# The net's weights are scanned in 88 pieces inside the attention units, from the inputs, and copied one matrix per chunk

## The chip, the cores and the metric

The kernel runs on one core of a Trainium2 chip. The metric is the time of the whole program in device microseconds; lower is better. The kernel uses four compute engines (PE for matmuls, DVE for vector work, ACT for activations, POOL for small vector work) and SP, which issues most DMAs in program order.

## What is computed

One transformer layer on x of 4096 x 256 in float32, 16 heads of 16 columns:

```python
q, k, v = x @ Wq.T + bq, x @ Wk.T + bk, x @ Wv.T + bv     # 16 heads of 16
q, k = rope(q), rope(k)
x = layernorm(x + softmax(q @ k.T / sqrt(256)) @ v @ Wo.T)
h = silu((x @ w1.T) * s1) * ((x @ w2.T) * s2)              # 256 -> 1024
h = gelu((h @ h1.T) * hs1)                                 # 1024 -> 1024
h = gelu((h @ h2.T) * hs2)                                 # 1024 -> 1024
x = layernorm(x + (h @ w3.T) * s3)                         # 1024 -> 256
```

The weights w1, w2, h1, h2 and w3 hold small whole numbers. The net has a fast form for weights whose low 12 bits are all zero and another for weights of any kind; the kernel looks at all the weights to choose.

## The kernel before

It has three blocks: `project`, `attend` and `feed_forward`. `attend` is the one that changes. It works in 32 units, u = c * NG + g: 8 chunks c of 512 queries times 4 groups g of 4 heads. One unit has 32 steps kt of 128 keys each.

PE does in a step, in this order (`unit`, L550): a pair of score matmuls (L572), two groups of "wide" matmuls (L507), another pair of score matmuls, and the sums over values of the step before (L532). The wide groups are not of the same unit: they compute scores of a later unit, from which DVE takes the maxima (L646), 64 groups (n = 0 to 63) a unit, two a step. `groups_beside` (L539) puts them LEAD = 6 steps ahead: beside step kt of unit u stand groups 2(kt + 6) and 2(kt + 6) + 1 of unit u + 1, and from kt = 26 on those of unit u + 2. A wide group n uses PSUM buffer n % 2 and waits (L504) until DVE has reduced group n - 2. Ahead of unit 0 PE computes all 64 groups of unit 0 and the first 12 of unit 1 with nothing beside them (L580 to L585).

After 64 groups DVE takes the top of each row (L655). PE turns it (L515), ACT negates it into `shift` (L617), POOL splits it (L474 to L485) and SP writes it as extra rows of `q_sb` (`place_shift`, L406), so that the score matmul subtracts the maximum. ACT takes exponentials of the scores (L624) and after the fourth of a unit copies the sums of the unit before to `mixed` (`take_sums`, L603).

Beside the attention the weights are looked through. SP first copies the five matrices to one DRAM buffer `w_dram` (L431, L432) and waits for all (L433). For each unit it loads a 32nd of it, 128 x 704 words, into `w_words` (`load_words`, L435), and DVE ORs the low bits into `bits` behind the unit's top reduction (`scan`, L662). At the end `bits` is reduced to `low_bits` (L680). `feed_forward` loads the weights from `w_dram` (L823).

SP's order in `attend` is: loads of q and of the last keys; two loads that fill the ones rows of `k_all` (L430, 384 KB each, 3 partitions each); the copies; `load_words(0)`, `place_shift(0)`; and then for each unit u:

```python
load_words(u + 1)       # waits for scan(u)
place_shift(u + 1)      # waits for POOL, near the end of unit u
finish(u)               # waits for ACT's take_sums(u), early in unit u + 1
load_q(c + 1, g)        # six DMAs; not in the last chunk
```

Of the kernel before, what the change touches and what calls it, by code (L numbers as in the profile page):

```python
# [19 lines left out]
I32 = mybir.dt.int32  # L20
ALU = mybir.AluOpType
# [3 lines left out]
P = 128  # L25
# [4 lines left out]
NCH = S // CH  # L30
# [7 lines left out]
LOW_BITS = 0xFFF  # L38


W_SHAPES = {"w1T": (D, HID), "w2T": (D, HID), "h1T": (HID, HID), "h2T": (HID, HID), "w3T": (HID, D)}
W_AT, W_TOTAL = {}, 0
for _name, (_rows, _cols) in W_SHAPES.items():
    W_AT[_name] = (W_TOTAL, _rows, _cols)
    W_TOTAL += _rows * _cols
INV_SCALE = 1.0 / float(D) ** 0.5


# [11 lines left out]
def place_k(sp, k_parts, k_all, c, ft, done):  # L60
    cols = bass.ds(c * CH, CH)
    pairs = slice(ft * PAIRS // FT, (ft + 1) * PAIRS // FT)
    for e in range(PAIR):
        for r, part in enumerate(K_PART):
            src = k_parts[part].rearrange("(j e d) s -> e d j s", e=PAIR, d=HD)[e]
            at = e * HALF + r * HD
            sp.dma_start(k_all[at:at + HD, pairs, cols].bitcast(F32), src[:, pairs, cols]).then_inc(done, 16)


def place_q(sp, q_parts, q_sb, c, g, done):  # L70
    for e in range(PAIR):
        for r, part in enumerate(Q_PART):
            src = q_parts[part].rearrange("(j e d) s -> e d j s", e=PAIR, d=HD)[e]
            at = e * HALF + r * HD
            sp.dma_start(q_sb[at:at + HD].bitcast(F32), src[:, g * GP:(g + 1) * GP, bass.ds(c * CH, CH)]).then_inc(done, 16)
# [251 lines left out]
def attend(nc, io, q_parts, k_parts, heads_dram, w_dram, low_bits, v_all, k_all):  # L327
# [6 lines left out]
    with ExitStack() as ctx:  # L334
        def sb(name, shape, dt=F32):
            return ctx.enter_context(nc.sbuf_tensor(name, shape, dt))

        def psum(name, shape):
            return ctx.enter_context(nc.psum_tensor(name, shape, F32))

        def sem(name):
            return ctx.enter_context(nc.semaphore(name))
# [6 lines left out]
        UNITS = NCH * NG  # L349
# [12 lines left out]
        shift_rest = sb("shift_rest", [QT, P])  # L362
        shift_parts = sb("shift_parts", [QT, 3, P], BF16)
        shift_rows = sb("shift_rows", [QT, 3, P], F32R)
        SCAN = W_TOTAL // P // UNITS
        w_words = sb("w_words", [P, SCAN], I32)
        bits = sb("bits", [P, SCAN], I32)
        scores = [psum(f"scores{b}", [P, CH]) for b in range(BANKS)]
        wide = [psum(f"wide{b}", [P, 2, CH]) for b in range(2)]
        sums = psum("sums", [P, CH])  # L370
# [9 lines left out]
        first_turn = sem("first_turn")  # L380
# [4 lines left out]
        exps_done = sem("exps_done")  # L385
        probs_free = sem("probs_free")
        w_copied = sem("w_copied")
        words_in = sem("words_in")
        scanned = sem("scanned")
        sums_free = sem("sums_free")  # L390
        mixed_free = [sem(f"mixed_free{p}") for p in range(2)]

        GROUPS = MAXG // KT

        def slot(n, turn=True):

            return n + 1 if turn and n >= TURN_AT else n
# [3 lines left out]
        @block.sync  # L401
        def _(sp):
            def load_q(c, g):
                place_q(sp, q_parts, q_sb[g], c, g, q_in[g])

            def place_shift(u, g):  # L406

                sp.wait_ge(part_step, (u + 2) * ROUNDS)
                for e in range(PAIR):
                    for a in range(3):  # L410
                        at = e * HALF + SHIFT_ROW + a
                        row = q_sb[g][at:at + 1].rearrange("o j (t s) -> o (j t) s", t=TT)
                        sp.dma_start(row.bitcast(F32), shift_rows[e * GP * TT:(e + 1) * GP * TT, a].bitcast(F32)).then_inc(shift_in, 16)

            def finish(c, g):

                sp.wait_ge(sums_free, c * NG + g + 2)
                sp.dma_start(heads_dram[bass.ds(c, 1), :, g].rearrange("c p s -> (c p) s"), mixed[g % 2][:])\
                    .then_inc(mixed_free[g % 2], 16)

            load_q(0, 0)
            place_k(sp, k_parts, k_all, NCH - 1, FT - 1, k_in)
            for g in range(1, NG):
                load_q(0, g)
            sp.wait_ge(ones_set, 1)
            for e in range(PAIR):
                at = e * HALF + SHIFT_ROW
                rows = k_all[at:at + 3].rearrange("a j (c s) -> a (j c) s", s=CH)
                src = mixed[0][0:3].unsqueeze(1).to_broadcast([3, PAIRS * NCH, CH])
                sp.dma_start(rows.bitcast(F32), src).then_inc(k_ones, 16)  # L430
            for name, (at, rows, cols) in W_AT.items():  # L431
                sp.dma_start(w_dram[at:at + rows * cols].rearrange("(r c) -> r c", c=cols), io[name]).then_inc(w_copied, 16)  # L432
            sp.wait_ge(w_copied, 16 * len(W_AT))  # L433

            def load_words(u):  # L435

                sp.wait_ge(scanned, u + 1)
                words = w_dram.bitcast(I32).rearrange("(u p n) -> u p n", u=UNITS, p=P)[bass.ds(u, 1)]
                sp.dma_start(w_words[:], words.rearrange("u p n -> (u p) n")).then_inc(words_in, 16)

            load_words(0)
            place_shift(0, 0)
            with sp.Fori(0, NCH - 1) as c:
                for g in range(NG):
                    load_words(c * NG + g + 1)
                    place_shift(c * NG + g + 1, (g + 1) % NG)
                    finish(c, g)
                    load_q(c + 1, g)
            for g in range(NG):
                if g < NG - 1:  # L450
                    load_words((NCH - 1) * NG + g + 1)
                    place_shift((NCH - 1) * NG + g + 1, g + 1)
                finish(NCH - 1, g)
            for p in range(2):
                sp.wait_ge(mixed_free[p], 16 + 16 * UNITS // 2)

        @block.gpsimd
        def _(pool):
# [37 lines left out]
        def _(pe):  # L496
# [42 lines left out]
            def groups_beside(c, g, kt, left):  # L539
# [7 lines left out]
                kt = (kt + LEAD) % KT  # L547
                return [(c, g, n) for n in range(kt * GROUPS, (kt + 1) * GROUPS)]

# [30 lines left out]
            for n in range(MAXG):  # L580
                max_group(0, 0, n)
            for n in range(LEAD * GROUPS):
                max_group(0, 1, n)
# [13 lines left out]
        def _(act):  # L597
# [12 lines left out]
            def unit(c, g, first=False, last=False):  # L610
                u = c * NG + g
                for n in range(TILES):
# [7 lines left out]
                    if n % HG == 0:  # L620

                        act.wait_ge(probs_free, u * KT + n // HG + 1)
                    act.wait_ge(scored, u * SLOTS + s + 1)
                    act.activation(probs[n % RING][:], scores[s % BANKS][:], ACT.Exp, scale=INV_SCALE)\  # L624
                        .then_inc(exps_done, 1)
# [11 lines left out]

        @block.vector
        def _(dve):
            def maxima(u):  # L640

                if not (isinstance(u, int) and u == 0):
                    dve.wait_ge(top_ready, u)
                for n in range(MAXG):
                    dve.wait_ge(wide_ready, u * MAXG + n + 1)
                    dve.reduce_max(group_max[:, n], wide[n % 2][:], AX_X).then_inc(wide_free, 1)  # L646
                dve.wait_ge(wide_free, (u + 1) * MAXG + 2)

                if isinstance(u, int):
                    if u == 1:  # L650
                        dve.wait_ge(first_turn, 1)
                else:
                    dve.wait_ge(scored, (u - 2) * SLOTS + TURN_AT + 1)
                by_head = group_max[:].rearrange("q (r b) e -> q e r b", b=NCH)
                dve.reduce_max(top[:].rearrange("q (e r) -> q e r", e=PAIR), by_head, AX_X).then_inc(top_ready, 1)  # L655

            for p in range(2):
                dve.sem_inc(mixed_free[p], 16)
            dve.sem_inc(wide_free, 2)
            dve.sem_inc(shift_in, 96)  # L660

            def scan(u):  # L662

                dve.wait_ge(words_in, u * 16 + 16)
                dve.wait_ge(scanned, u + 1)
                dve.scalar_tensor_tensor(out=bits[:], in0=w_words[:], scalar=LOW_BITS, in1=bits[:],
                                         op0=ALU.bitwise_and, op1=ALU.bitwise_or).then_inc(scanned, 1)

            dve.memset(bits[:], 0).then_inc(scanned, 1)
            maxima(0)  # L670

            dve.memset(sums[:], 0.0).then_inc(sums_free, 1)
            scan(0)
            maxima(1)
            scan(1)
            with dve.Fori(2, UNITS) as u:
                maxima(u)
                scan(u)
            dve.wait_ge(scanned, UNITS + 1)
            dve.reduce_max(low_bits[:], bits[:], AX_X).then_inc(scanned, 1)  # L680
            dve.wait_ge(scanned, UNITS + 2)


def feed_forward(nc, io, heads_dram, shares_dram, w_dram, low_bits, out):
# [562 lines left out]
```

## Time and profile before

| | us |
|---|---|
| median of 3 runs (3811.04 to 3815.56) | 3811.35 |
| the profiled execution | 3821.48 |
| its span, first to last instruction | 3819.9 |
| PE busy | 3526.6 (92%) |
| DVE busy | 2932.8 (77%) |
| ACT busy | 2462.1 (64%) |
| POOL busy | 196.4 (5%) |
| mean granted clock of PE | 0.948 |

In a row of the page or of a list of groups, "L646 DVE TENSOR_REDUCE group_max<-wide" is a line of the kernel, the engine, the operation, and what it writes and reads; then come the shapes, the count, the busy time, the mean of one in ns, and the idle time of the engine just before it with what ended it. A timeline is a list of instructions in order of time, several of a kind merged into one row. PEld is PE's weight load, SPq and POOLq are the queues' own issuing of DMAs. A granted clock of 1.00 is 2.4 GHz, 0.50 is 1.2 GHz.

### The profile page before, as it was taken

Reading aid. Unit: us, or ns where it says so; the run is one execution under the profiler, and the core shown is the slowest. Engines: PE = TensorE matmul, PEld = TensorE weight load, DVE = VectorE, ACT = ScalarE, POOL = GpSimd, SP = SyncE. Lnnn points to the kernel's source line nnn. Section 1 sums busy time; section 2 is a strip of 40 time slices with the busy share of each in tenths; the row PEclk is TensorE's granted clock in tenths of the full one; section 3 lists DMA queues with packets and bytes.
Section 4 is the critical chain, followed back from the end, with each engine's and each line's share of the span. In section 5 each row is a group of like instructions: output and inputs, shape, how many; then the busy total and the mean of one; then the engine's idle time right before and its main releaser. Section 6 shows DMA issues by size and latency. Waiting matters only on the chain. (4 is left out here: it accounts for less than half of the span.)

```text
span 3819.9 us, 63480 instructions
## 1 busy us (share of the span) xinstructions
PE 3526.6 (92%) x20130; PEld 1516.0 (40%) x20130; DVE 2932.8 (77%) x3148; ACT 2462.1 (64%) x4472; POOL 196.4 (5%) x352
## 2 busy tenths in 40 slices
PE   8569999999999999999999999999998869999999
PEld 3223333333333333332333333333332158888887
DVE  6698999899899989998998999899983035555554
ACT  2118888788888878888887888788886512222222
POOL 3200000000000000000000000000000011111100
PEclk9759999999999999999999999999997589999999
DMA  8940000000000000000000000000000051111100
GB/s 208 212 137 12 12 12 12 13 12 12 23 12 12 12 13 12 12 12 17 18 12 13 12 12 12 12 12 23 8 8 4 3 182 35 34 34 44 40 17 12
DMA packets 64516, 125.61 MB, mean 33 GB/s; under 512 B 12551, under 2 KB 24904, under 8 KB 63032
## 3 DMA queue, kind: packets, MB, share of 16 engines
q1 hardware_dynamic: 59528, 114.02, 10.6%
q0 software_dynamic: 4704, 7.81, 0.7%
q8 instruction: 177, 2.90, 0.3%
q14 instruction: 107, 0.88, 0.1%
HBM read 90.59 MB, written 41.16 MB: 34 GB/s over the span
## 5 line engine op out<-in xcount | busy, mean ns | idle before, releaser
L646 DVE TENSOR_REDUCE group_max<-wide 128x2 f32<-128x1024 f32 x2048 | 2406.0, 1219 | 277.9 <-PE wide L507 277.6
L624 ACT ACTIVATE probs<-scores 128x512 f32<-128x512 f32 x4096 | 2223.3, 595 | 524.6 <-PE scores L572 431.5
L572 PE MATMUL scores<-q_sb,k_all 51*128 51x512 f32 x4096 | 1053.5, 511 | 148.6 <-ACT probs L624 62.7
L532 PE MATMUL sums<-probs,v_all 128*17 128x512 f32 x8192 | 1117.7, 619 | 0.0
L572 PEld LDWEIGHTS scores<-q_sb,k_all 51*128 51x128 f32 x4096 | 391.7, 188 | 1384.3 <-ACT probs L624 1355.7
L507 PE MATMUL wide<-k_all,q_sb 48*128 48x512 f32 x4096 | 807.3, 459 | 76.3 <-DVE group_max L646 50.2
L507 PEld LDWEIGHTS wide<-k_all,q_sb 48*128 48x128 f32 x4096 | 397.9, 191 | 394.8 <-DVE group_max L646 363.8
L1029 ACT ACTIVATE whole_hid<-acc,scale 128x512 f32<-128x512 f32 x128 | 84.6, 688 | 346.8 <-PE acc L910 346.7
L910 PE MATMUL acc<-hid_b,h2T 128*128 128x512 f32 x1024 | 241.6, 397 | 0.0
L910 PE MATMUL acc<-hid_a,h1T 128*128 128x512 f32 x1024 | 240.2, 395 | 0.0
L532 PEld LDWEIGHTS sums<-probs,v_all 128*17 128x17 f32 x8192 | 137.4, 96 | 258.2 <-ACT probs L624 150.7
L910 PEld LDWEIGHTS acc<-hid_b,h2T 128*128 128x128 f32 x1024 | 193.0, 188 | 45.7
L910 PEld LDWEIGHTS acc<-hid_a,h1T 128*128 128x128 f32 x1024 | 191.9, 187 | 47.1
L1119 DVE CAST hid_a<-whole_hid 128x512 fp32r<-128x512 f32 x128 | 54.5, 426 | 185.5 <-ACT whole_hid L1029 183.3
L474 POOL CAST shift_parts<-shift 16x128 bf16<-16x128 f32 x32 | 9.1, 283 | 2654.4 <-ACT shift L617 2575.8
L1020 ACT ACTIVATE gate<-acc,scale 128x512 f32<-128x512 f32 x64 | 44.1, 688 | 124.5 <-PE acc L910 120.1
L1180 DVE TENSOR_SCALAR flag<-flip 1x1 int32<-1x1 f32 x1 | 0.1, 146 | 157.9 <-PE flip L997 157.9
L227 PE MATMUL ps_qk<-xt,w_qk 128*128 128x512 f32 x128 | 72.4, 729 | 27.9 <-DMA xt<-in_xT 27.9
L1121 DVE TENSOR_TENSOR hid_a<-whole_hid,hid_a 128x512 fp32r<-128x512 f32 x128 | 88.6, 693 | 4.4
L1128 DVE SCALAR_TENSOR_TENSOR whole_hid<-acc,scale,gate 128x512 f32<-128x512 f32 x64 | 48.0, 751 | 44.5 <-PE acc L910 44.4
L883 PE MATMUL tok<-wo,heads_sb 128*128 128x256 f32 x256 | 59.5, 393 | 17.8 <-DVE heads_sb L1094 17.8
L910 PE MATMUL acc<-x1t,w1T 128*128 128x512 f32 x256 | 71.0, 399 | 2.1 <-DVE x1t L1113 2.1
(77 smaller groups left out, 1156.9 us busy)
## 6 DMA issues: line engine op xcount, KB each, us to landing
k_all<-k_parts SPq DMA_DIRECT2D x96, 128.0 KB, 5.0
q_sb<-q_parts SPq DMA_DIRECT2D x192, 64.0 KB, 2.3
w_words<-ff_weights SPq DMA_DIRECT2D x32, 352.0 KB, 3.1
q_parts<-parts SPq DMA_DIRECT2D x16, 512.0 KB, 5.6
k_parts<-parts SPq DMA_DIRECT2D x16, 512.0 KB, 6.2
heads<-mixed SPq DMA_DIRECT2D x32, 256.0 KB, 2.5
heads_sb<-heads SPq DMA_DIRECT2D x8, 1024.0 KB, 4.9
shares<-shares_dram POOLq DMA_DIRECT2D x112, 64.0 KB, 2.3
```

The lines of the kernel that those rows point to most:

```text
L227: last = pe.matmul(ps[m][:], w_sb[:, t, i, ft * P:(ft + 1) * P], xt[p][:, i], start=(i == 0), stop=(i == FT - 1))
L507: last = pe.matmul(wide[n % 2][:, e], q_sb[g][rows, j, t * P:(t + 1) * P], k_all[rows, g * GP + j, b * CH:(b + 1) * CH], start=True, stop= ...
L532: last = pe.matmul(sums[32 * j:32 * j + HD + 1, :], v_all[:, g, kt, j], probs[(kt * HG + j) % RING][:], start=(kt == 0), stop=(kt == KT - 1))
L572: pe.matmul(scores[(s + e) % BANKS][:], k_all[rows, g * GP + j, kt * P:(kt + 1) * P], q_sb[g][rows, j], start=True, stop=True).then_inc(sc ...
L624: act.activation(probs[n % RING][:], scores[s % BANKS][:], ACT.Exp, scale=INV_SCALE)\
L646: dve.reduce_max(group_max[:, n], wide[n % 2][:], AX_X).then_inc(wide_free, 1)
L883: last = pe.matmul(tok[t // 2][:, t % 2], heads[:, g, t * P:(t + 1) * P], wo[:, g], start=(g == 0), stop=(g == NG - 1))
L910: mm = pe.matmul(dst, w.bitcast(view), src[h].bitcast(view), start=(first and h == 0), stop=(last and h == 1))
L1029: act.activation(whole[o % 4][:], acc[n % 4][:], ACT.Gelu, scale=scale[:, 2 + layer, o:o + 1])\
L1119: dve.tensor_copy(dst[0][:, k % HT], whole[k % 4][:]).then_inc(rounded, 1)
L1121: dve.tensor_tensor(dst[1][:, k % HT], whole[k % 4][:], dst[0][:, k % HT].bitcast(F32), ALU.subtract)\
L1128: dve.scalar_tensor_tensor(out=whole[o % 4][:], in0=acc[(2 * o + 1) % 4][:], scalar=scale[:, 1, o:o + 1], in1=gate[o % 2][:], op0=ALU.mult ...
```

## The change

The words that DVE scans are loaded from the inputs, not from the DRAM copy, in 88 pieces of 128 x 256 words, 2 or 3 to a unit. Two buffers `w_words` take turns; the load of piece i waits for the scan of piece i - 2. The scans move from behind the top reduction to behind reductions 12, 32 and 52 of a unit's maxima. The five copies to `w_dram` move from the start to SP's work for chunks 1 to 5, one each, behind `load_q` for g = 0, and SP waits for them at its end. The loops of SP and DVE over the units are written out instead of being loops of the program.

```diff
+PIECE = 256
+PIECES = [(name, n) for name, (rows, cols) in W_SHAPES.items() for n in range(rows * cols // (P * PIECE))]
...
-        SCAN = W_TOTAL // P // UNITS
-        w_words = sb("w_words", [P, SCAN], I32)
-        bits = sb("bits", [P, SCAN], I32)
+        w_words = [sb(f"w_words{p}", [P, PIECE]) for p in range(2)]
+        bits = sb("bits", [P, PIECE], I32)
...
-        words_in = sem("words_in")
+        words_in = [sem(f"words_in{p}") for p in range(2)]
...
+        def pieces_beside(u):
+            return range(len(PIECES) * u // UNITS, len(PIECES) * (u + 1) // UNITS)
...
-            for name, (at, rows, cols) in W_AT.items():
-                sp.dma_start(w_dram[at:at + rows * cols].rearrange("(r c) -> r c", c=cols), io[name]).then_inc(w_copied, 16)
-            sp.wait_ge(w_copied, 16 * len(W_AT))
 
             def load_words(u):
 
-                sp.wait_ge(scanned, u + 1)
-                words = w_dram.bitcast(I32).rearrange("(u p n) -> u p n", u=UNITS, p=P)[bass.ds(u, 1)]
-                sp.dma_start(w_words[:], words.rearrange("u p n -> (u p) n")).then_inc(words_in, 16)
+                for i in pieces_beside(u):
+                    name, n = PIECES[i]
+                    if i >= 2:
+
+                        sp.wait_ge(scanned, i)
+                    words = io[name].rearrange("r c -> (r c)").rearrange("(n p w) -> n p w", p=P, w=PIECE)[n]
+                    sp.dma_start(w_words[i % 2][:], words).then_inc(words_in[i % 2], 16)
 
             load_words(0)
             place_shift(0, 0)
-            with sp.Fori(0, NCH - 1) as c:
+            for c in range(NCH - 1):
                 for g in range(NG):
                     load_words(c * NG + g + 1)
                     place_shift(c * NG + g + 1, (g + 1) % NG)
                     finish(c, g)
                     load_q(c + 1, g)
+                    if 0 < c <= len(W_AT) and g == 0:
+                        name, (at, rows, cols) = list(W_AT.items())[c - 1]
+                        sp.dma_start(w_dram[at:at + rows * cols].rearrange("(r c) -> r c", c=cols), io[name]).then_inc(w_copied, 16)
...
+            sp.wait_ge(w_copied, 16 * len(W_AT))
...
+            def scan(i):
+
+                dve.wait_ge(words_in[i % 2], 16 * (i // 2) + 16)
+                dve.wait_ge(scanned, i + 1)
+                dve.scalar_tensor_tensor(out=bits[:], in0=w_words[i % 2][:].bitcast(I32), scalar=LOW_BITS, in1=bits[:],
+                                         op0=ALU.bitwise_and, op1=ALU.bitwise_or).then_inc(scanned, 1)
+
             def maxima(u):
...
                 for n in range(MAXG):
                     dve.wait_ge(wide_ready, u * MAXG + n + 1)
                     dve.reduce_max(group_max[:, n], wide[n % 2][:], AX_X).then_inc(wide_free, 1)
+                    if n % 20 == 12 and n // 20 < len(pieces_beside(u)):
+                        scan(pieces_beside(u)[n // 20])
...
             maxima(0)
 
             dve.memset(sums[:], 0.0).then_inc(sums_free, 1)
-            scan(0)
-            maxima(1)
-            scan(1)
-            with dve.Fori(2, UNITS) as u:
+            for u in range(1, UNITS):
                 maxima(u)
-                scan(u)
```

## Rows read from the trace of the kernel before

**Rows 1.** Windows by stage: busy PE, PEld, DVE, ACT, POOL, granted clock, DMA share, GB/s.

```profile
170.00:254.00 84.00, 52.41 (x133) 19.09 (x133) 73.90 (x67) 0.27 (x1) 1.30 (x4) 0.50 0.67 182
...
270.00:2905.00 2635.00, 2493.99 (x15827) 806.16 (x15823) 2353.39 (x2037) 2167.61 (x4013) 57.90 (x154) 0.99 0.05 13
2905.00:3057.00 152.00, 121.73 (x438) 26.13 (x438) 0.00 (x0) 79.36 (x146) 0.68 (x2) 0.50 0.01 4
```

**Rows 2.** Timeline from unit 2's first step: start, length, engine, line, [idle before].

```profile
441.91 0.51 PE L572 MATMUL scores<-q_sb,k_all 51*128 51x512 f32 x2
...
442.25 0.75 PE L507 MATMUL wide<-k_all,q_sb 48*128 48x512 f32 x4
...
442.51 0.19 PEld L507 LDWEIGHTS wide<-k_all,q_sb 48*128 48x128 f32 x2 [0.30 <-DVE group_max L646]
442.69 2.35 DVE L646 TENSOR_REDUCE group_max<-wide 128x2 f32<-128x1024 f32 x2 [0.24 <-PE wide L507]
...
443.10 0.50 PE L572 MATMUL scores<-q_sb,k_all 51*128 51x512 f32 x2
...
444.51 0.50 PE L572 MATMUL scores<-q_sb,k_all 51*128 51x512 f32 x2
...
444.65 0.60 ACT L608 ACTIVATE mixed<-sums 128x512 f32<-128x512 f32 x1
...
448.94 0.35 SPq L439 DMA_DIRECT2D w_words<-ff_weights  x1
```

**Rows 3.** Timeline of the start of the attention, rows of DVE and SP.

```profile
173.74 2.65 SPq L75 DMA_DIRECT2D q_sb<-q_parts  x6
...
179.48 72.48 DVE L646 TENSOR_REDUCE group_max<-wide 128x2 f32<-128x1024 f32 x64 [4.48 <-PE wide L507]
...
188.08 1.78 SPq L430 DMA_DIRECT2D k_all<-mixed  x2
...
189.90 13.85 SPq L432 DMA_DIRECT2D ff_weights<-in_w1T  x1
```

**Rows 4.** The same timeline: the first scan and the reductions behind it.

```profile
256.98 0.89 DVE L666 SCALAR_TENSOR_TENSOR bits<-w_words,bits 128x704 int32<-128x704 int32 x1 [4.10 <-DMA w_words<-ff_weights]
257.79 15.92 DVE L646 TENSOR_REDUCE group_max<-wide 128x2 f32<-128x1024 f32 x14
```

**Rows 5.** Windows of that start; the last two columns are DMA share and GB/s.

```profile
192.00:204.00 12.00, 8.56 (x22) 3.16 (x22) 12.00 (x12) 0.00 (x0) 0.00 (x0) 0.50 0.18 26
204.00:240.00 36.00, 25.24 (x66) 9.22 (x64) 36.00 (x33) 0.00 (x0) 0.00 (x0) 0.50 0.94 313
240.00:252.00 12.00, 8.33 (x22) 2.91 (x20) 11.97 (x11) 0.00 (x0) 0.00 (x0) 0.50 0.14 60
```

**Rows 6.** A group of DVE's by line, and a scan in the timeline of unit 3.

```profile
L1101 DVE TENSOR_TENSOR x<-tok,x_sb 128x256 f32<-128x256 f32 x32 | 11.4, 416 | 9.4 <-PE tok L883 9.4
...
510.40 0.89 DVE L666 SCALAR_TENSOR_TENSOR bits<-w_words,bits 128x704 int32<-128x704 int32 x1
...
511.20 4.61 DVE L646 TENSOR_REDUCE group_max<-wide 128x2 f32<-128x1024 f32 x4
```

**Rows 7.** Timeline in the last chunk, and the page's DMA issue of q.

```profile
2746.61 0.60 ACT L608 ACTIVATE mixed<-sums 128x512 f32<-128x512 f32 x1
...
2747.66 0.43 SPq L439 DMA_DIRECT2D w_words<-ff_weights  x1
...
q_sb<-q_parts SPq DMA_DIRECT2D x192, 64.0 KB, 2.3
```

**Rows 8.** First scores behind a turn of PE's loop, and a window of the clock.

```profile
697.18 0.80 PE L572 MATMUL scores<-q_sb,k_all 51*128 51x512 f32 x2 [2.73 <-issue]
...
701.21 0.79 PE L572 MATMUL scores<-q_sb,k_all 51*128 51x512 f32 x2
...
697.20:707.20 10.00, 10.00 (x40) 3.64 (x40) 5.39 (x5) 6.03 (x11) 0.00 (x0) 0.50 0.26 72
```

**Rows 9.** The tile of the words: issue to landing of its 32 loads.

```profile
DMA to landing us min/median/max: 2.8/3.1/4.0
```

More of the change, by code:

```diff
@@ L639, in _ @@
         def _(dve):
+            def scan(i):
[3 more added lines that the diff above has]
+                                         op0=ALU.bitwise_and, op1=ALU.bitwise_or).then_inc(scanned, 1)
             def maxima(u):
-                if not (isinstance(u, int) and u == 0):
+                if u > 0:
                     dve.wait_ge(top_ready, u)
@@ L646, in maxima @@
                     dve.reduce_max(group_max[:, n], wide[n % 2][:], AX_X).then_inc(wide_free, 1)
+                    if n % 20 == 12 and n // 20 < len(pieces_beside(u)):
+                        scan(pieces_beside(u)[n // 20])
                 dve.wait_ge(wide_free, (u + 1) * MAXG + 2)
[L649 to L652, printed above, removed]
+                if u == 1:
+                    dve.wait_ge(first_turn, 1)
+                elif u > 1:
                     dve.wait_ge(scored, (u - 2) * SLOTS + TURN_AT + 1)
@@ L660, in _ @@
             dve.sem_inc(shift_in, 96)
[L662 to L667, printed above, removed]
             dve.memset(bits[:], 0).then_inc(scanned, 1)
@@ L672, in _ @@
             dve.memset(sums[:], 0.0).then_inc(sums_free, 1)
-            scan(0)
-            maxima(1)
-            scan(1)
-            with dve.Fori(2, UNITS) as u:
+            for u in range(1, UNITS):
                 maxima(u)
-                scan(u)
-            dve.wait_ge(scanned, UNITS + 1)
+            dve.wait_ge(scanned, len(PIECES) + 1)
             dve.reduce_max(low_bits[:], bits[:], AX_X).then_inc(scanned, 1)
-            dve.wait_ge(scanned, UNITS + 2)
+            dve.wait_ge(scanned, len(PIECES) + 2)
 def feed_forward(nc, io, heads_dram, shares_dram, w_dram, low_bits, out):
```

## The prediction

> **What bounds the kernel now.** I read the profile in the order of its stages, first as windows [rows 1]: 170 to 254 us is the maxima of unit 0, with 67% of DMA time used; from 270 to 2905 us the units with maxima beside them run, PE, DVE and ACT all busy for 82 to 95%, DMA 5%; from 2905 to 3057 us what is left of the attention runs without maxima at half clock; then comes the net. The change touches the first two stages. So the question is which wait ends last there.
>
> In a unit 32 steps of 2.60 us repeat (441.91 to 444.51). [Rows 2] are one, the first of unit 2 (S0 below is its first score pair): score pair, two groups of "wide" matmuls, score pair, sums. No engine is plainly the bound; they form a ring. The second wide group waits for DVE's reduction of the group two before (0.30), DVE then waits 0.24 for PE. The second wide pair ends at 443.00 and the score pair behind it starts at 443.10, so some 0.1 us of lateness is free; beyond that a late reduction delays everything, and nothing later gives it back. In the maxima of unit 0 it is simpler: 64 reductions in 72.48 us, 1.13 each, one DVE chain [rows 3].
>
> **First part: the five copies leave the start, and the first piece is asked for there.** Before, SP issued the copies from 189.90 on [rows 3] and loaded the first words only when they had landed. DVE waited 4.1 us for those words and scanned for 0.81 until its next reduction could begin at 257.79 [rows 4]. Both disappear from that place, a gain of 4.9.
>
> But `scan(0)` now stands behind reduction 12 of unit 0, so DVE wants piece 0 at 179.48 + 13 x 1.13 = 194.2. SP comes to that load at 189.90 at the earliest, right behind the two loads of the ones rows into `k_all` (188.08). Those are 2 x 384 KB. From 192 to 204 the DMA share is 0.18 of 16 engines, which is three engines, at 26 GB/s [rows 5]: 0.79 MB at that rate lasts some 31 us from 190, to about 221. The load issued next (w1T's copy) needed 13.85 us for its issue alone, although 13 engines were free [rows 3]. And the last copies end on a share of 0.14, two engines working on alone from 240 to 252 although every copy is spread evenly [rows 5]: what is issued behind the ones rows waits, on the engines that carry them, until they are through. Taking a piece's load as spread over all engines, as the copies were, piece 0 is whole only at about 223. DVE stands from 194.2 to 223; the delay is 29.1 with the scan (0.34, below), and `scan(1)` adds 0.34 in this DVE chain: 29.5. Bounds: 0.7, the scans alone, if the load slips past; 31 if the pieces land late. I take the row of the engine share. Unit 0 starts 29.5 - 4.9 = **25 us later** (range 22 to 27; -4 at the other bound), since PE must do twelve groups of unit 1 before unit 0, and those follow DVE at 1.13 each.
>
> **Second part: the scans themselves.** A scan of 704 columns takes 0.89 us and holds DVE for 0.80 (510.40 to 511.20) [rows 6]. Elementwise work of 256 columns takes 0.416 [rows 6], so a piece takes 0.42 and, with the same 0.08 of overlap, holds DVE for 0.34. Its place is behind reductions 12, 32 and 52, all even, which is between the two reductions of a step: 0.34 less the free 0.1 is 0.24 each. A unit has 2.75 pieces; the one at 12 is in the third part, the other 1.75 cost 0.4. The scan behind the top reduction disappears: of its 0.80 the ring's 0.1 was free, so I credit 0.7 (0.4 to 0.8). Sum: **-0.3 a unit**. The last reduction over `bits` runs beside PE.
>
> DVE's and SP's loops become straight code. The scan's hold on DVE is 0.80 in the loop (510.40 to 511.20) and 0.81 ahead of it (256.98 to 257.79) [rows 4, 6], so I give nothing for that. The Trainium skill (Runtime: NRT & Kernel Launch, Instruction fetch mechanics) says that a taken branch can stall for a fetch and that kernels prefer unrolling where they can. The trace shows such a stall on PE (2.73 us before its loop's first scores at 697.18 [rows 8]), whose loop stays; by the page DVE would gain, by the rows it gains nothing.
>
> **Third part: who has the words when DVE asks.** This is the large term. SP works in order: words of unit u+1, shift of u+1, `finish(u)`, six `load_q`. So the words for the maxima of unit u+1 are issued only after `finish(u-1)` and its six loads, and `finish(u-1)` waits for ACT's `take_sums`, early in unit u. PE runs the maxima LEAD = 6 steps ahead, so groups 12 and 13 of unit u+1 are those of the very first step of unit u. Before, the words were wanted at that maxima's end, about 60 us later. Now they are wanted at reduction 12. From S0 (441.91) [rows 2]: reduction 13 would start at 442.69 + 1.14, +1.9. ACT's `mixed` starts at +2.74; in the last chunk, straight code without `load_q`, the words' issue follows 1.05 later (2746.61, 2747.66 [rows 7]); six loads of q take 2.65 [rows 3]: piece 0 is issued at +6.4 (before, in the loop, +7.0: 448.94 [rows 2]). Landing: 352 KB took 2.8 to 4.0, 64 KB 2.3 [rows 7, 9]; for 128 KB I take 2.6: +9.0. Scan 0.34 and a wait: reduction 13 starts at +9.4, **7.5 late**, 7.4 on the ring. Wide group 15 needs its bank, and behind it on PE stand all scores and sums, on those ACT. `take_sums` comes before the block, so nothing deadlocks, and it repeats in every unit. Bounds: 7.0 to 8.6.
>
> After such an idle PE runs at half clock. At a turn of its loop PE was idle for 2.73 us; the granted clock from 697.2 to 707.2 is then 0.50, that is 1.2 GHz, and a step takes 4.03 us instead of 2.60 (697.18 to 701.21) [rows 8]. In 10 us that is 2.5 steps instead of 3.8, 3.5 us lost at most; one slow step, 1.4, is the least. The new idle is over twice as long, so I take the fall as certain: 2.6 (1.7 to 3.3).
>
> A unit so costs 7.4 + 2.6 - 0.3 = 9.7. It holds for the maxima of units 2 to 29, 28 x 9.7 = **272** (8.3 to 11.4 each: 232 to 319; the ends are the sums of those of the stall, the clock and the scans). Those of units 30 and 31 have no `load_q` ahead (issue at +3.9 instead of +6.4): 4.8 + 2.6 - 0.3 = 7.1 each, **14**. Unit 1's words are issued behind the first shift and come in time.
>
> **Fourth part: one copy a chunk.** It is issued behind `load_q` of g = 0, so right ahead of the words that DVE stands waiting for. The five moved 11.5 MB at 313 GB/s while all engines worked (204 to 240 [rows 5]), 3.4 us a MB: 3.4 for each of w1T, w2T and w3T, 13 for h1T and h2T. The pieces stand behind them on all engines, so five stalls grow by 36, and by some 0.5 of issue each: **38** (28 to 50).
>
> **Sum.** 25 + 272 + 14 + 38 = 349. The profiled execution took 3821.5 us around a span of 3819.9, the median of the runs is 3811.35; none of the terms depends on that difference: 3821 + 349 = 4170 in a profile, and **4160** as median.
>
> **Rivals.**
> - Words in time (not slower): if SP's chain were short enough that piece 0 lands before +1.9, every stall goes; then -4 at the start, and -0.7 + 2.75 x 0.24, about 0, per unit: 3806. It decides at a landing 7.1 us earlier than worked out; the issue alone is at +6.4. 2%.
> - The stall without the clock's loss: if PE came back at full clock, 28 x 7.1 + 9 + 63 = 271: 4082. Against it: at the turn in [rows 8] a shorter idle did bring the half clock. 6%.
> - The clock stays at half once fallen, as it did from 2905 on [rows 1]: with 4.03 for 2.60 over 30 units, 1380 more, 5500. Against it: with wide groups beside, the mean granted clock over 270 to 2905 is 0.99, so it came back after each turn. 2%.
> - The first piece doesn't wait for the ones rows: 29 less, 4131, inside the range. 8%.
> - The tail (152 us at half clock) stays at full clock: it holds the last 6 steps of unit 30 and the 32 of unit 31, 38 in 152 us, 4.0 each; at 2.6 it is 53 less, 4107. 4%.
> - The forecast: 78%.
>
> **Range.** Low ends: 22 + 232 + 11 + 28 = 293; high ends: 27 + 319 + 18 + 50 = 414. That is 4104 to 4225; I go down to 4080, which takes in the cases of the clock without loss, the first piece and the tail, and up to 4240 for a stall that brings both long landings and long half clocks. Words in time and a clock that stays at half are left out. A difference under 0.2% (7.6 us) can't be told from no change. Faster 1%, same 2%, slower 97%.
>
> **What would show it.** Right: DVE's `bits` waits for DMA `w_words` 30 times, some 7 us (over 15 with h1T and h2T) and once 29 us at 194; PE idle at `wide` behind DVE; the granted clock at 0.50 once a unit for 6 to 10 us; units of 94 us instead of 84.1; the first `finish`, `load_q`, words order on SP as before. Wrong: no DMA ahead of `bits`, units within 1 us of 84, or PE's clock unchanged between 280 and 2905.

## The result, and the profile after

The changed kernel takes 4138.66 us, median of 4 runs (4131.16 to 4152.28), where the kernel before takes 3811.68 on the same occasions: ratio 1.086, interval 1.083 to 1.089. The forecast was 4160 (4080 to 4240). The profiled execution has a span of 4138.6 us beside 3819.9 before, 318.7 us more, with a mean granted clock of 0.910 instead of 0.948.

The page after: slices of PE, DVE, granted clock and DMA, and the group of the scans.

```profile
PE   8568888888988879887888888888898859999999
...
DVE  6588888788877867886888788788888115554454
...
PEclk8659999899999988998999999999999659999999
DMA  8800000000000010001000000000000032110010
...
L653 DVE SCALAR_TENSOR_TENSOR bits<-w_words,bits 128x256 int32<-128x256 int32 x88 | 36.9, 419 | 273.8 <-DMA w_words<-in_h1T 107.4
```

All three engines of the ring (PE, DVE and ACT) are busy for 87, 71 and 59% of the span instead of 92, 77 and 64; none has become the bound. The 88 scans are 36.9 us of work, but DVE stood idle 273.8 us ahead of them, waiting for `w_words`. The waits view splits this by the matrix the words come from:

```profile
DVE bits L653 <- DMA w_words<-in_h1T: 107.4, 12, 21.9
...
DVE bits L653 <- DMA w_words<-in_h2T: 102.2, 12, 21.0
```

With the others there are 31 waits: 30, one a unit, as expected, and the first.

**The start.** SP's issues, the first scan, and a window, answering [rows 3, 5]; the bracket is the idle time ahead.

```profile
188.13 17.71 SPq L444 DMA_DIRECT2D w_words<-in_w1T  x2
...
220.70 0.43 DVE L653 SCALAR_TENSOR_TENSOR bits<-w_words,bits 128x256 int32<-128x256 int32 x1 [27.83 <-DMA w_words<-in_w1T]
...
188.00:222.00 34.00, 4.04 (x12) 1.44 (x10) 6.17 (x7) 0.00 (x0) 0.00 (x0) 0.50 0.22 37
```

Two loads of 128 KB take 17.7 us to issue. The first has landed when DVE scans it, 32.6 us after its issue, on a DMA share of 0.22; the only other loads issued just ahead are those of the ones rows.

**A unit.** The timeline of unit 3's start, answering [rows 2] (the score pair at 475.40 is the unit's first), and the clock behind the stall.

```profile
475.40 0.50 PE L581 MATMUL scores<-q_sb,k_all 51*128 51x512 f32 x2
...
478.14 0.60 ACT L617 ACTIVATE mixed<-sums 128x512 f32<-128x512 f32 x1
...
478.76 0.35 SPq L422 DMA_DIRECT2D heads<-mixed  x1
479.16 2.77 SPq L77 DMA_DIRECT2D q_sb<-q_parts  x6
481.97 3.01 SPq L444 DMA_DIRECT2D w_words<-in_w2T  x3
484.20 0.42 DVE L653 SCALAR_TENSOR_TENSOR bits<-w_words,bits 128x256 int32<-128x256 int32 x1 [6.79 <-DMA w_words<-in_w2T]
484.54 3.48 DVE L662 TENSOR_REDUCE group_max<-wide 128x2 f32<-128x1024 f32 x3
485.81 0.80 PE L516 MATMUL wide<-k_all,q_sb 48*128 48x512 f32 x2 [7.07 <-DVE group_max L662]
...
484.20:492.00 7.80, 6.08 (x30) 2.10 (x32) 5.84 (x6) 3.26 (x6) 0.00 (x0) 0.65 0.07 17
```

Here the whole chain can be read off: `mixed` at +2.7 us, the store of it, six loads of q, the words at +6.6, their landing at +8.8, the scan, and PE, idle for 7.07 us until reduction 13 frees the bank of wide group 15. Its pair then takes 0.80 instead of 0.40, at half clock.

**A unit with a copy.** The same order in chunk 3, with h1T's 4 MB between the loads of q and the words.

```profile
1524.20 3.00 SPq L77 DMA_DIRECT2D q_sb<-q_parts  x6
1527.24 0.56 SPq L456 DMA_DIRECT2D ff_weights<-in_h1T  x1
1527.85 16.10 SPq L444 DMA_DIRECT2D w_words<-in_h1T  x3
1543.17 0.42 DVE L653 SCALAR_TENSOR_TENSOR bits<-w_words,bits 128x256 int32<-128x256 int32 x1 [21.91 <-DMA w_words<-in_h1T]
```

**Where the 318.7 us are.** I take the start of a unit from its first score pair. Unit 0 begins at 291.96 instead of 269.83, 22.1 later. From there to unit 31 it takes 2945.1 instead of 2650.7 us, 294.4 more. From unit 31 to the net 138.4 in both, and the net 2.1 more. The 294.4 are 45 for the five copies (in the maxima of units 6, 10, 14, 18 and 22 DVE stands 5.0 to 5.5 us longer behind 1 MB and 14.2 to 15.1 longer behind 4 MB than in the others, where wait and scan are 7.2), 9 in the last two stalls, 2 in unit 0, and 238 in the 28 units with an ordinary stall, 8.5 each.

### The profile page after: what moved, and what is told of

The parts are those of the page before. It is cut to its first block and busy times, and to the rows that moved or that the text cites. A ratio compares the mean times of both kernels' runs of the same rounds, so it can differ in the third digit from the quotient of the medians.

```text
span 4138.6 us, 61164 instructions
## 1 busy us (share of the span) xinstructions
PE 3592.9 (87%) x20130; PEld 1530.1 (37%) x20130; DVE 2936.6 (71%) x3204; ACT 2459.3 (59%) x4472; POOL 197.2 (5%) x352
## 5 line engine op out<-in xcount | busy, mean ns | idle before, releaser
L581 PE MATMUL scores<-q_sb,k_all 51*128 51x512 f32 x4096 | 1069.7, 519 | 139.1 <-ACT probs L633 59.7
L541 PE MATMUL sums<-probs,v_all 128*17 128x512 f32 x8192 | 1155.8, 638 | 0.0
L516 PE MATMUL wide<-k_all,q_sb 48*128 48x512 f32 x4096 | 838.2, 468 | 336.3 <-DVE group_max L662 310.6
L581 PEld LDWEIGHTS scores<-q_sb,k_all 51*128 51x128 f32 x4096 | 401.5, 193 | 1400.1 <-ACT probs L633 1371.7
L516 PEld LDWEIGHTS wide<-k_all,q_sb 48*128 48x128 f32 x4096 | 410.7, 197 | 663.8 <-DVE group_max L662 631.7
L653 DVE SCALAR_TENSOR_TENSOR bits<-w_words,bits 128x256 int32<-128x256 int32 x88 | 36.9, 419 | 273.8 <-DMA w_words<-in_h1T 107.4
```

The lines of the kernel that those rows point to most:

```text
L516: last = pe.matmul(wide[n % 2][:, e], q_sb[g][rows, j, t * P:(t + 1) * P], k_all[rows, g * GP + j, b * CH:(b + 1) * CH], start=True, stop= ...
L541: last = pe.matmul(sums[32 * j:32 * j + HD + 1, :], v_all[:, g, kt, j], probs[(kt * HG + j) % RING][:], start=(kt == 0), stop=(kt == KT - 1))
L581: pe.matmul(scores[(s + e) % BANKS][:], k_all[rows, g * GP + j, kt * P:(kt + 1) * P], q_sb[g][rows, j], start=True, stop=True).then_inc(sc ...
```

## The experiments

The theory (A): DVE stands because each unit's words are asked for 7 us before they can land, and PE, whose clock falls meanwhile, loses some more behind it; copies and ones rows ahead of the words make it longer. Rivals: scans between the reductions cost something of their own; the straight code does; the copies disturb PE wherever they run; the slow steps behind a stall are not the clock's. Ratios are to the kernel before, run beside each on the same chip, whose median there was 3814.5 to 3818.1 us. As it was 3811.68 beside the changed kernel, a difference of medians and one of ratios can be some 10 us apart. A turn of PE's loop, once in four units, makes one or two units longer; where I compare units I take those from 1 to 28 without it, 84.1 to 84.25 us each before.

### Words loaded earlier

```diff
             place_shift(0, 0)
+            load_words(1, slice(0, 2))
             for c in range(NCH - 1):
                 for g in range(NG):
-                    load_words(c * NG + g + 1)
+                    load_words(c * NG + g + 1, slice(2, None))
                     place_shift(c * NG + g + 1, (g + 1) % NG)
+                    load_words(c * NG + g + 2, slice(0, 2))
```

> The changed kernel with one thing moved: the loads of the first two pieces of unit u+2 are issued right behind the shift of unit u+1, about one step before unit u+1 begins; the third piece and the copies stay where they are. Theory A (DVE stands because each piece is asked for 7 us before it lands): no wait of bits for w_words but the first (28 us at 193), no half clock in the units, units of 83.7 us; 22 us from the start, about -0.46 per unit for the scan that left the top reduction: 3820 (3812 to 3830). Theory B (the scans between the reductions cost by themselves, or the straight code does): most of the 327 us stays, over 4000.

Measured: 3825.6 us, ratio 1.0023 (1.0012 to 1.0033). Units without a turn of PE's loop take 83.6 to 83.8 us. Three views of it: the waits ahead of `bits`, a window of the units, and the timeline of unit 2 around its scan behind reduction 12:

```profile
DVE bits L657 <- DMA w_words<-in_w1T: 27.8, 1, 27.8
...
300.00:2900.00 2600.00, 2467.65 (x15734) 796.28 (x15726) 2341.78 (x2078) 2149.67 (x3986) 56.84 (x150) 0.99 0.06 17
...
467.07 0.41 DVE L657 SCALAR_TENSOR_TENSOR bits<-w_words,bits 128x256 int32<-128x256 int32 x1
...
467.75 0.50 PE L585 MATMUL scores<-q_sb,k_all 51*128 51x512 f32 x2
...
468.68 0.50 PE L520 MATMUL wide<-k_all,q_sb 48*128 48x512 f32 x2 [0.19 <-DVE group_max L666]
...
470.43 0.50 PE L585 MATMUL scores<-q_sb,k_all 51*128 51x512 f32 x2
```

All 30 waits in the units are gone, the first one stays, and the granted clock is 0.99 as before [rows 1]. The same 88 pieces, scans and straight code are there, so it was neither of them: 313 us hung on when the loads are issued. The scan makes reduction 13 start 0.33 us late and the second wide pair behind it wait 0.19, yet that step takes 2.68 us (467.75 to 470.43), as the same step of unit 2 does before (2.69).

### Scans further back

```diff
-                    if n % 20 == 12 and n // 20 < len(pieces_beside(u)):
-                        scan(pieces_beside(u)[n // 20])
+                    if n >= 22 and (n - 22) % 20 == 0 and (n - 22) // 20 < len(pieces_beside(u)):
+                        scan(pieces_beside(u)[(n - 22) // 20])
```

> The changed kernel with the scans behind reductions 22, 42 and 62 instead of 12, 32 and 52; loads and copies as they are. 22 is reduced 13 to 14 us behind the unit's first scores, 4.5 behind the landing. Theory A: no wait in ordinary units; with the five copies ahead of the words 1 us for 1 MB and 10 us for 4 MB remains; at the start DVE asks at 204.5 for what lands at 220.5, so 16 instead of 28: 3811 + 11 - 14 + 27 = 3835 (3825 to 3850). Theory B: over 4000, as the same scans stand in the same stream.

> As with 22, but behind reductions 23, 43 and 63, the second of a step. The prediction's ring (0.1 us free between the two reductions, so 0.24 for each scan behind an even one): 0.15 to 0.24 less for each of 88 scans, so 13 to 20 us faster than with 22, and 1 us a copy less. Rival, after the trace of the changed kernel, where the steps with scans behind 32 and 52 took 2.60 us as the others: the place within a step makes no difference, so within 4 us of the kernel with 22.

Measured: 3831.49 us behind 22, ratio 1.0032 (1.0022 to 1.0043), and 3830.32 behind 23, ratio 1.0036 (1.0021 to 1.0050). What is left of the waits behind 22:

```profile
DVE bits L653 <- DMA w_words<-in_w1T: 16.9, 1, 16.9
...
DVE bits L653 <- DMA w_words<-in_h1T: 7.7, 1, 7.7
DVE bits L653 <- DMA w_words<-in_h2T: 6.9, 1, 6.9
```

The loads are untouched and now come in time, except behind a 4 MB copy and at the start. Together with the experiment before it, this is the cause from both of its sides. Between even and odd places the medians differ by 1 us and the ratios the other way, within their intervals, where the ring of the prediction wanted 13 to 20 us; units without a turn or a wait take 83.6 to 83.8 us in both. That part of the prediction falls. The steps of unit 10 with the scans behind 22, 42 and 62 take 2.60 us as the others do.

### The first words ahead of the ones rows

```diff
+            load_words(0)
             sp.wait_ge(ones_set, 1)
             for e in range(PAIR):
                 at = e * HALF + SHIFT_ROW
...
-            load_words(0)
             place_shift(0, 0)
```

> The changed kernel with the loads of pieces 0 and 1 issued ahead of the two loads of the ones rows of k_all instead of behind them. Theory A (pieces are stuck on the engines that carry the ones rows): the wait of 27.8 us at 193 goes, 28 us less than the changed kernel, 4110 (4102 to 4120). Rival (the first piece was late for its own issue or for the load of the DMA engines with the q loads, which are still ahead of it): less than 10 us gained.

Measured: 4104.22 us, ratio 1.0755 (1.0727 to 1.0782), 34 less than the changed kernel. SP's issues and the first scan:

```profile
186.60 0.90 SPq L437 DMA_DIRECT2D w_words<-in_w1T  x2
187.54 1.78 SPq L445 DMA_DIRECT2D k_all<-mixed  x2
...
193.19 0.42 DVE L653 SCALAR_TENSOR_TENSOR bits<-w_words,bits 128x256 int32<-128x256 int32 x1
```

The same two loads are now issued in 0.90 instead of 17.71 us and the scan waits for nothing, with the q loads ahead of it as before. Unit 0 begins at 264.4 instead of 292.0, which is 27.5 of the gain. For the rest I have no cause; the runs of the changed kernel lie 21 us apart and those of this one 22.

### The copies moved

```diff
                     place_shift(c * NG + g + 1, (g + 1) % NG)
+                    if 0 < c <= len(W_AT) and g == 1:
+                        ...
                     finish(c, g)
                     load_q(c + 1, g)
-                    if 0 < c <= len(W_AT) and g == 0:
-                        ...
```

> The changed kernel with the five copies issued behind the shift of g = 1, near the end of that unit, instead of right ahead of the words that DVE stands waiting for. In the changed kernel the five units with a copy wait 5.1, 5.0, 5.0 us (1 MB) and 15.0, 14.2 us (4 MB) longer than the others, 44 in all. Theory A (the words queue behind the copy): up to 44 less, some of it kept because 4 MB are still under way when the next words are issued: 4098 (4090 to 4110). Rival (the copies slow PE or its instruction fetch wherever they run): no gain, 4139.

Measured: 4099.53 us, ratio 1.0729 (1.0705 to 1.0753), 39 less than the changed kernel. Its four runs lie between 4083 and 4131, so the size of the gain is uncertain, and the profiled one was the slowest, so I read only its waits: the longest for h1T is 11.4 instead of 21.9, for h2T 11.0 instead of 21.0. That the copies cost by standing ahead of the words, and not by running, is shown better by the version below with all three causes away: there they run in the same places, no scan waits, and the units in which they start (85 to 86 us) are no longer than before.

### The loops written out, alone

```diff
-            with sp.Fori(0, NCH - 1) as c:
+            for c in range(NCH - 1):
...
-            with dve.Fori(2, UNITS) as u:
+            for u in range(2, UNITS):
```

> The kernel before with nothing changed but the two loops, SP's over the chunks and DVE's over the units, written out as straight code. The rows of before (a scan holds DVE 0.80 us in the loop and 0.81 ahead of it): no difference, ratio 1.000 (0.998 to 1.002). Rival (a taken branch costs a fetch, 31 turns of DVE's loop and 7 of SP's): faster by 5 us or more.

Measured: 3815.69 us, ratio 0.9999 (0.999 to 1.0008). Straight code is worth nothing here, although the Trainium skill (Runtime: NRT & Kernel Launch, Instruction fetch mechanics) speaks for it: turning the loops of DVE and SP held nothing up that could be measured. PE's loop was not written out in any run, so what holds PE for 2.73 us at its turn [rows 8] is not shown.

### PE kept busy in the stall

```diff
-                for e in range(PAIR):
+                beside = not (isinstance(c, int) and c == 0 and g < 2)
+                for e in list(range(PAIR)) * (16 if n == 14 and beside else 1):
```

> The changed kernel, but PE repeats the pair of matmuls of wide group 14 sixteen times in every unit from unit 2 on; that group stands just ahead of the one at which PE is held up, so PE works through most of the 7 us in which it sat idle, and the result of the group is the same. Theory A (about 2 us of each stall's 8.5 are the half clock behind it): the granted clock stays at 1.00 in most units, 30 to 70 us less than the changed kernel, 4090. Rival (the slow steps behind the stall come from the restart of the ring, not from the clock): no gain, 4139 or more, although the clock stays up.

Measured: 4148.49 us, ratio 1.0875 (1.0859 to 1.0892), where 30 to 70 us less than the changed kernel had been expected. It decides nothing between the two theories, since the clock didn't stay up: in unit 3 the repeats took 0.21 us a pair, some 3.3 us in all, PE was idle for 4.4 more, and the clock fell all the same. So the second try, with 34.

> With 16 repeats of wide group 14 PE worked only 3.3 us of the 7 (pairs ran at 0.21 us) and the clock fell all the same. Now 34 repeats, 7.2 us, which fill an ordinary stall. Theory A (about 2 us of each stall are the half clock behind it): the granted clock stays at 1.00 behind the ordinary stalls, not behind the five with a copy; 30 to 60 us less than the changed kernel, 4090. Rival (restart of the ring): no gain, 4139 or more, although the clock stays up.

Measured: 4089.01 us, ratio 1.0702 (1.0683 to 1.0721), 50 less than the changed kernel. The stretch of unit 3 behind the stall, and the units together:

```profile
479.68 3.14 PE L517 MATMUL wide<-k_all,q_sb 48*128 48x512 f32 x26
480.50 0.43 DVE L654 SCALAR_TENSOR_TENSOR bits<-w_words,bits 128x256 int32<-128x256 int32 x1 [6.76 <-DMA w_words<-in_w2T]
...
484.20:492.00 7.80, 7.29 (x50) 2.20 (x48) 7.34 (x7) 6.42 (x12) 0.00 (x0) 1.00 0.01 2
...
300.00:3050.00 2750.00, 2595.15 (x17031) 958.10 (x17031) 2251.30 (x1995) 2065.32 (x3829) 54.92 (x145) 0.98 0.06 16
```

DVE still waits 6.76 us, but the granted clock stays at 1.00 (2.4 GHz), where it was 0.65 behind the same stall after. Over 300 to 3050 us it is 0.98 instead of 0.93. From unit 0 to unit 31 it takes 2895.1 us instead of 2945.1. Most units without a turn take 90.7 to 90.8 us instead of 92.0 to 95.3. So the clock's share is shown: 50 us of the 319 (60 by the ratios), at least, since behind the stalls with a copy the clock still fell; and what is left is a stall of 7.1 us a unit (90.8 less 83.7).

### All three causes away

The first kernel here has the scans behind 23, 43 and 63, the first words ahead of the ones rows, and the copies behind the shift of g = 1. The second leaves out the loads of words and the scans as well.

> The changed kernel with all three causes of its stalls taken away: the first two pieces are loaded ahead of the ones rows, the scans stand behind reductions 23, 43 and 63, the copies behind the shift of g = 1. Theory A: start 5 us earlier than before (264.4 instead of 269.8 for the first scores), units of 83.7 instead of 84.15, and the rest as before: ratio 0.995 (0.993 to 0.997), some 3798. Rival (scans in the stream of reductions cost something of their own, 88 x 0.24 = 21 us): ratio 1.000 or more.

> The kernel with all three causes taken away (3801 us, ratio 0.996), and with the 88 loads of words and the 88 scans left out as well, so the weights are not looked through at all. If scans between the reductions are free, as the 2.60 us steps of the changed kernel say: the same within 3 us, ratio 0.996. If each costs the 0.24 us of the prediction's ring: 21 us less, ratio 0.990.

Measured: with all three away 3801.37 us, ratio 0.9961 (0.9947 to 0.9974), so this version beats both kernels. Without any scan 3794.88 us, ratio 0.994 (0.9927 to 0.9954). The scans of the first of them, from its list of groups:

```profile
L653 DVE SCALAR_TENSOR_TENSOR bits<-w_words,bits 128x256 int32<-128x256 int32 x88 | 36.6, 416 | 0.0
```

No idle time is left ahead of them. In its profile unit 0 begins at 263.9 instead of 269.8, units 0 to 30 take 2636.1 instead of 2650.7, and the rest is the same: 20 us in the profile, 13 to 15 in the medians. The two kernels' ratios are 0.0021 apart, 8 us, and their intervals overlap a little: more than the 3 us expected of free scans, less than the 21 us of the prediction's ring, and even the far ends of the two intervals are only 18 us apart. The profiles, whose spans differ by 0.6 us, have units of 83.8 to 83.9 and 83.7 to 83.8, 2 us over all. So the scans and their loads together cost little, and whether exactly nothing isn't settled.

### The large scan moved, alone

```diff
                     dve.reduce_max(group_max[:, n], wide[n % 2][:], AX_X).then_inc(wide_free, 1)
+                    if n == 23 and not (isinstance(u, int) and u == 0):
+                        scan(u)
...
                 maxima(u)
-                scan(u)
```

> The kernel before with one thing moved: from unit 1 on, the scan of 704 columns stands behind reduction 23 of a unit's maxima instead of behind the top reduction; its words land 4 to 5 us earlier than that. Theory A (behind the top reduction DVE has no slack, within a step it has about 0.3 us): the step at the turn goes from 3.55 to 3.09 us, the step with the scan gives back less than that, 5 to 14 us faster than before, ratio 0.998. Rival (0.80 us in one piece is more than a step can hide): same or slower, ratio 1.000 to 1.003; then the small pieces are what makes the scan free, not its place.

Measured: 3806.91 us, ratio 0.9975 (0.9965 to 0.9985). The step with the scan in unit 3, then the step of that unit in which PE turns the tops of the rows (L515; below, the top's step). The first scores of each, with those of the next step:

```profile
546.29 0.50 PE L572 MATMUL scores<-q_sb,k_all 51*128 51x512 f32 x2
...
549.00 0.50 PE L572 MATMUL scores<-q_sb,k_all 51*128 51x512 f32 x2
...
598.33 0.50 PE L572 MATMUL scores<-q_sb,k_all 51*128 51x512 f32 x2
...
601.43 0.50 PE L572 MATMUL scores<-q_sb,k_all 51*128 51x512 f32 x2
```

The top's step of unit 2 before, where the scan of 0.80 us stands just ahead (510.40 in [rows 6]):

```profile
512.10 0.49 PE L572 MATMUL scores<-q_sb,k_all 51*128 51x512 f32 x2
...
515.65 0.50 PE L572 MATMUL scores<-q_sb,k_all 51*128 51x512 f32 x2
```

The step with a scan that holds DVE for 0.80 us takes 2.71 instead of 2.60, the top's step 3.10 instead of 3.55. So about 0.7 us of a scan behind an odd reduction is hidden, not 0.1, and the place alone, without pieces, brings 0.25% of the 0.39% that the pieces in good places bring with the earlier start.

## Why the prediction was right

The mechanism was worked out before the run, and its waits came where it had put them; one step of it, the price of a late reduction, failed. The sum was 30 us too high (349 forecast, 318.7 in the profile), mostly by the clock's term.

- **The start: 25 forecast, 22.1 measured.** DVE waited 27.83 us at reduction 12 for a piece behind the ones rows. It came at 220.7, not 223: the estimate of their end from 26 GB/s, about 221, was good, and the two I added to it were not needed. Loading the words first takes the whole wait away.
- **The scans between the reductions: +0.4 a unit forecast, 0 measured in the steps** (the medians leave room for 8 us over all). This is the step that failed: "some 0.1 us of lateness is free; beyond that a late reduction delays everything, and nothing later gives it back". With a scan behind reduction 12, reduction 13 started 0.33 us late and the step was no longer; steps with scans take 2.60 us; even and odd places don't differ; a scan of 0.80 us costs 0.1. The 0.1 was read off a row of four merged matmuls. By how much a late reduction can run into the next steps before PE has lost time, no run measured.
- **The scan gone from behind the top reduction: -0.7 forecast, -0.46 measured** (the top's step went from 3.55 to 3.09). Together -0.5 instead of -0.3 a unit.
- **The stall: reduction 13 at +9.4 forecast, +9.2 measured** (9.07 to 9.30 in the units with neither copy nor turn). The order of SP, taken from the code, and the distances from the rows made this term; the landing I had put at 2.6 had a median of 2.2. On the ring 7.4 were forecast and 7.1 measured.
- **The clock: 2.6 forecast, 1.3 in the least disturbed units** (92.1 less 90.8), and 1.8 on the mean of 28 by the 50 us that keeping PE busy gave back. The fall itself was right. At 14 of the 30 stalls the half clock lasted 6.8 us or less, much of it while PE was idle anyway; at 11 it lasted 10 to 17 us and at the five with a copy 17 to 34, and ordinary units then took up to 95.3 us. I had priced all stalls by 10 us of a busy PE, as in [rows 8].
- **A unit: 9.7 forecast, 8.5 measured**, so 272 became 238; the last two 9 instead of 14.
- **The copies: 38 forecast, 45 measured.** 3.4 and 13 us were the transfer alone; the waits grew by 5 and 14 to 15, a little less than a copy's time from issue to landing in this kernel (5.6 to 5.8 and 15.2 to 15.6).
- **Straight code: 0 forecast, 0 measured.**
- **The range.** The high end of a unit, 11.4, isn't the sum of its parts: 8.6 + 3.3 + 0 is 11.9, so 28 units come to 333 and the high end to 4239, which the 4240 just takes in. The low end of the clock (1.7) and the bounds of the copies (28 to 50) were given without working.

The rival of a stall without the clock's loss was the nearest, 4082; the run that took most of that loss away by keeping PE busy gave 4089. What stays open: why the half clock lasts longer behind some stalls, and why unit 0 and the net took 2 us more each.

## What to carry to other kernels

When work is moved to an earlier place, look up what issues its data and what that issuer waits for ahead of it: here the words were requested behind a store that waited for the same unit's start, so no placement before +9 us could be free. A transfer issued ahead of yours on the same queue can go into your wait: here 5 us for a copy of 1 MB, 15 for one of 4 MB, 28 for two loads onto three partitions each. And where three engines form a ring, a wait of 7 us on one was paid by all nearly in full (7.1), with 1.3 and more on top for PE's clock.

## What the runs showed of the hardware

- Behind two loads of 384 KB that write three partitions each, a load of 128 KB landed only 33 us after they were issued (DMA share 0.22 of 16 engines, 37 GB/s), and even its issue was held: 17.71 us for two such loads behind them, 0.90 ahead of them.
- Repeated matmul pairs of 48 rows ran at 0.21 us a pair. In unit 3, where 3.3 us of them were followed by 4.4 us of idle PE, the granted clock fell to 0.50 (1.2 GHz); where they filled the wait it stayed at 1.00 (2.4 GHz).
- An extra 0.80 us of DVE in a step of 2.60 us, in which its two reductions take 2.35, cost 0.1: the idle time ahead of them (0.24) was no measure of the slack.
